# Start of a fused FFN, attention, FFN block: first block of tokens normalised alone, weight flag from raw bits, one branch instead of two

## The reference

```python
def _L0_ffn_ref(x, w1_w, w1_s, w2_w, w2_s, h1_w, h1_s, h2_w, h2_s, w3_w, w3_s):
    h = silu(_tlin(x, w1_w, w1_s)) * _tlin(x, w2_w, w2_s)      # 128 -> 512
    h = gelu(_tlin(h, h1_w, h1_s))                             # 512 -> 512
    h = gelu(_tlin(h, h2_w, h2_s))                             # 512 -> 512
    return _tlin(h, w3_w, w3_s)                                # 512 -> 128
x = x + 0.5 * ffn(layernorm(x))
x = x + attention(layernorm(x))        # 16 heads of 8, softmax over 256 keys
x = x + 0.5 * ffn(layernorm(x))
```

## Time and profile before

| What | us |
|---|---|
| three executions | 636.6, 638.17, 639.28 (median 638.17) |
| the profiled execution, its own time | 636.52 |
| its span | 634.7 |
| TensorE busy | 597.0 (94%) |
| ScalarE busy | 466.7 (74%) |
| VectorE busy | 436.8 (69%) |
| GpSimd busy | 94.7 (15%) |

### The profile page before, as it was taken

One profiled execution on the slowest core, in us unless ns is written; L12 is line 12 of the kernel. 1 busy time (PEld: TensorE's weight loads), 2 busy tenths in 40 slices (PEclk: granted clock), 3 DMA queues, 4 the chain that ended last, 5 costly groups with the idle time before them and its releaser, 6 DMA issues.

```text
span 634.7 us, 12980 instructions
## 1 busy us (share of the span) xinstructions
PE 597.0 (94%) x4452; PEld 437.7 (69%) x4452; DVE 436.8 (69%) x1034; ACT 466.7 (74%) x793; POOL 94.7 (15%) x258
## 2 busy tenths in 40 slices
PE   1959999999999999999999999999899999999996
PEld 0738878878776675656656565666578878788785
DVE  4845485667835687979889898896385666855742
ACT  2746796787875568787878878787587877977964
POOL 2702001021010311222222222012001020020000
PEclk9979999999999979999999999999899999999999
DMA  8200000000034073434437062400000001000011
GB/s 287 69 2 2 0 1 1 2 0 0 1 133 133 24 242 124 144 136 133 165 104 263 36 229 106 162 2 2 3 2 0 1 1 35 0 6 27 1 33 35
DMA packets 36674, 41.97 MB, mean 66 GB/s; under 512 B 2448, under 2 KB 27280, under 8 KB 36624
## 3 DMA queue, kind: packets, MB, share of 16 engines
q1 hardware_dynamic: 36624, 41.31, 19.3%
HBM read 22.42 MB, written 18.87 MB: 65 GB/s over the span
## 4 chain that ended last, share of the span: by engine, by line
PE 76%; DVE 8%; issue 7%; POOL 3%; ACT 3%; DMA 2%; POOLq 0%; SPq 0%; DVEq 0%; ACTq 0%
PE bank L1021 48%; PE bank L1129 7%; PE bank L1104 6%; PE bank L1116 3%; PE bank L1118 2%; DVE neg_max L832 2%; PE bank L1161 2%; PE bank L1086 1%; PE bank L1090 1%; DVE act_lo L782 1%; PE bank L1068 1%; PE bank L1147 1%; PE bank L1139 1%; DMA QK<-qk_scratch 1%; DVE silu L791 1%
## 5 line engine op out<-in xcount | busy, mean ns | idle before, releaser
L1021 PE MATMUL bank<-act_hi,WH 128*128 128x512 f32 x576 | 233.1, 405 | 6.6 <-issue 5.3
L1021 PE MATMUL bank<-act_lo,WH 128*128 128x512 f32 x576 | 228.3, 396 | 0.0
L832 DVE TENSOR_REDUCE neg_max<-bank 128x2 f32<-128x512 f32 x256 | 166.2, 680 | 31.8 <-PE bank L1104 30.2
L802 DVE TENSOR_TENSOR act_lo<-full,act_hi 128x512 fp32r<-128x512 f32 x128 | 87.8, 688 | 123.2 <-ACT act_hi L536 123.0
L647 ACT ACTIVATE probs<-bank 128x512 f32<-128x512 f32 x256 | 139.3, 597 | 34.1 <-PE bank L1118 32.3
L534 ACT ACTIVATE full<-bank,SG 128x512 f32<-128x512 f32 x128 | 88.1, 688 | 70.0 <-PE bank L1021 69.6
L1021 PEld LDWEIGHTS bank<-act_hi,WH 128*128 128x128 f32 x576 | 108.7, 189 | 36.8 <-issue 5.9
L1021 PEld LDWEIGHTS bank<-act_lo,WH 128*128 128x128 f32 x576 | 108.8, 189 | 25.1 <-issue 0.5
L1116 PE MATMUL bank<-QK 32*128 32x256 f32 x512 | 93.1, 331 | 0.9 <-DVE m_parts L838 0.5
L536 ACT ACTIVATE act_hi<-bank,SG 128x512 fp32r<-128x512 f32 x128 | 87.4, 683 | 0.0
L1118 PE MATMUL bank<-m_parts,SEL 32*128 32x256 f32 x512 | 79.3, 277 | 0.0
(11 more groups left out here) (91 smaller groups left out, 593.2 us busy)
## 6 DMA issues: line engine op xcount, KB each, us to landing
qk_scratch<-qk SPq DMA_DIRECT2D x64, 256.0 KB, 2.6
QK<-qk_scratch SPq DMA_DIRECT2D x16, 1024.0 KB, 7.1
X<-x SPq DMA_DIRECT2D x4, 512.0 KB, 7.2
raw_rest<-w_ffn SPq DMA_DIRECT2D x4, 512.0 KB, 6.0
out<-X SPq DMA_DIRECT2D x4, 512.0 KB, 3.2
raw<-w_ffn SPq DMA_DIRECT2D x3, 256.0 KB, 4.5
WA<-w_att SPq DMA_DIRECT2D x1, 256.0 KB, 5.4
xT<-sel SPq DMA_DIRECT2D x1, 256.0 KB, 5.4
```

The source lines that it names most:

```text
L802: D.tensor_tensor(act_lo[1 + layer][:, j, t, :], full[:, t, :], act_hi[1 + layer][:, j, t, :].bitcast(F32), op=ALU.subtract)\
L832: D.tensor_reduce(neg_max[:, bb, qt, n0:n0 + 2], bank[(banks or A_BANKS[bb])[u]][:, :].rearrange("p (h k) -> p h k", h=2), axis=AX.X, op=A ...
L1021: ins = MM(dst, a, b, start=k == 0, stop=k == len(todo) - 1)
```

## The change

1. **x in halves.** The first pair of x comes in two DMAs of 256 KB, `x_in` and `x_second_in`.
2. **Block 0 alone.** VectorE makes the statistics and the guess of block 0 (4 tiles of tokens), then runs its three Newton rounds itself (`first_newton`, 9 operations: the fused `scalar_tensor_tensor` does two of the four steps), with the statistics of block 1 written in between. GpSimd's Newton is for block 1 only. Block 1 is normalised after block 0's low part, and TensorE transposes it after the second tile of `layer1`.
3. **Flag from raw bits.** `low_bits(k)` takes the largest magnitude of the low 16 bits of each fp32 weight, read as int16 with a step of two, from the raw weights. It waits for the DMA of the group only. The matmul that sums it stands after tile 6 of `layer1`, ahead of tile 7.
4. **GpSimd's low parts later.** It starts them when 4 tiles of `act_lo` are made (`h_lo`), and ScalarE waits for them ahead of the second hidden layer. `raw_rest` moves to the place of that layer's output.
5. **ScalarE's order.** `weight_hi` of groups 2 and 3 comes ahead of block 0's `split_x`, groups 4 to 6 and block 1's `split_x` after it.
6. **One branch.** Both FFN phases and attention stand in one function, `all_layers`, written twice; the two-matmul form comes first, and the branch is not taken when the flag is 0.

```diff
-            load_x(0, x_in)
+            for j, arrived in ((0, x_in), (1, x_second_in)):
+                sp.dma_start(X[:, TT * j:TT * j + TT, :], x_t[:, TT * j:TT * j + TT, :]).then_inc(arrived, 16)
...
-            rsqrt_steps(0, 0)
+            rsqrt_steps(0, 0, TT, TT)
+            pool.wait_ge(h_lo, HT)
             for k in range(2, len(W_GROUPS)):
                 pool.wait_ge(w_hi, k + 1)
...
+                    if f == 0 and first:
+                        act.wait_ge(w_lo_rest, len(W_GROUPS) - 2)
                     hidden(g + 2 * HT, 1, 0)
...
                     weight_hi(0)
                     weight_hi(1)
+                    weight_hi(2)
+                    weight_hi(3)
                     split_x(nb, 0)
-                    weight_hi(2)
-                    split_x(nb + 1, 1)
-                    weight_hi(3)
+                    weight_hi(4)
                     act.wait_ge(consts_in, 16 * N_CONSTS)
-                    layer1(t1, {t: lambda k=t + 4: weight_hi(k) for t in range(3)})
+                    layer1(t1, {0: lambda: weight_hi(5), 1: lambda: split_x(nb + 1, 1), 2: lambda: weight_hi(6)})
...
-            def weight_lo_max(k):
-                if k < 2:
-                    dve.wait_ge(w_lo, k + 1)
-                else:
-                    dve.wait_ge(w_lo_rest, k - 1)
-                D.tensor_reduce(lo_max[:, k:k + 1], part_of(WL, k).bitcast(F32), axis=AX.XY, op=ALU.max,
-                                apply_absolute_value=True).then_inc(lo_reduced, 1)
+            def low_bits(k):
+                dve.wait_ge(w_in[k], 16)
+                halves = raw_of(k).bitcast(I16).rearrange("p k (c t) -> p k c t", t=2)
+                D.tensor_reduce(low_max[:, k:k + 1], halves[:, :, :, 0], axis=AX.XY, op=ALU.max,
+                                apply_absolute_value=True).then_inc(bits_reduced, 1)
...
+            def first_newton(it, step):
+                v, y, a = var_m[:, 0:TT], rstd[:, 0:TT], newton[:, 0:TT]
+                if it == 0 and step == 0:
+                    dve.wait_ge(first_guess, 1)
+                else:
+                    dve.wait_ge(first_step, 3 * it + step)
+                if step == 0:
+                    ins = D.tensor_tensor(a, y, y, op=ALU.mult)
+                elif step == 1:
+                    ins = D.tensor_tensor(a, a, v, op=ALU.mult)
+                else:
+                    ins = D.scalar_tensor_tensor(out=y, in0=a, scalar=1.5, in1=y, op0=ALU.add, op1=ALU.mult)
+                ins.then_inc(first_rstd if (it, step) == (NEWTON - 1, 2) else first_step, 1)
...
-                    side = {t: lambda k=t + 2: weight_lo_max(k) for t in range(5)}
-                    layer1(t1, side | {5: all_lo_max, 6: take_flag})
+                    layer1(t1, {0: lambda: low_bits(3), 1: lambda: low_x(nb + 1, 1), 2: lambda: low_bits(4),
+                                3: lambda: low_bits(5), 4: lambda: low_bits(6), 5: all_low_bits, 6: take_flag})
...
+            def all_layers(general):
+                pe.wait_ge(w_hi, len(W_GROUPS))
+                if general:
+                    pe.wait_ge(w_lo_rest, len(W_GROUPS) - 2)
+                ffn_bodies(0, general)
...
+                ffn_bodies(1, general)
...
+            transpose_x(0, 0)
+            pe.wait_ge(w_lo, 2)
+            layer1(0, 0, True, {1: lambda: transpose_x(1, 1), 6: sum_low_bits})
+            pe.wait_ge(flag_set, 1)
+            pe.reg_load(low_weights, flag[0:1, 0:1].bitcast(I32))
+            with pe.If_eq(low_weights, 0):
+                all_layers(False)
+            with pe.Else():
+                all_layers(True)
```

More of the change, by code:

```diff
@@ L24 @@
 F32R = mybir.dt.float32r
+I16 = mybir.dt.int16
 I32 = mybir.dt.int32
@@ L156, in macaron_kernel @@
         x_in = sem("x_in")
+        x_second_in = sem("x_second_in")
         x_rest_in = sem("x_rest_in")
@@ L730, in take_flag, with norm_steps @@
                 D.tensor_copy(flag[:, :], bank[6][0:1, 0:1]).then_inc(flag_set, 1)
-            def norm_steps(n, tile0, width=8, biased=0):
+            def norm_steps(n, tile0, width=8, biased=0, at=0, sems=None):
+                done = sems or (stats_done, moments_done, var_done, half_done, guess_done)
+                cols = slice(at, at + width)
                 def s_stats():
@@ L755, in s_half @@
+                    D.tensor_scalar(var_m[:, cols], moments[:, cols, 1], EPS, -0.5, ALU.add, ALU.mult)
+                    D.tensor_scalar(var[:, cols], moments[:, cols, 1], EPS, None, ALU.add).then_inc(done[2], 1)
                 def s_half():
-                    dve.wait_ge(var_done, n + 1)
-                    D.tensor_scalar(half[:, 0:width], var[:, 0:width].bitcast(I32), 1, None,
-                                    ALU.arith_shift_right).then_inc(half_done, 1)
+                    dve.wait_ge(done[2], n + 1)
@@ L760, in s_guess @@
+                    D.tensor_scalar(half[:, cols], var[:, cols].bitcast(I32), 1, None,
+                                    ALU.arith_shift_right).then_inc(done[3], 1)
                 def s_guess():
-                    dve.wait_ge(half_done, n + 1)
-                    D.tensor_scalar(rstd[:, 0:width].bitcast(I32), half[:, 0:width], -1.0,
-                                    float(RSQRT_MAGIC), ALU.mult, ALU.add).then_inc(guess_done, 1)
+                    dve.wait_ge(done[3], n + 1)
+                    D.tensor_scalar(rstd[:, cols].bitcast(I32), half[:, cols], -1.0,
+                                    float(RSQRT_MAGIC), ALU.mult, ALU.add).then_inc(done[4], 1)
@@ L769, in normalise @@
+            def normalise(n, tile0, t0, width=4, ready=None):
+                dve.wait_ge(ready or rstd_done, n + 1)
                 for t in range(t0, t0 + width):
@@ L1244, in ffn_bodies, with sum_low_bits @@
                 body(NP - 1, more=False)
[L1246 to L1270 removed]
+            def sum_low_bits():
+                pe.wait_ge(ones_set, 1)
+                pe.wait_ge(bits_reduced, len(W_GROUPS) + 1)
+                MM(bank[6][0:1, 0:1], ONES[:, 0:1], low_max[:, len(W_GROUPS):len(W_GROUPS) + 1],
+                   start=True, stop=True).then_inc(flag_sum, 1)
             def attend(b, pair, par, bb, prev=True, prev2=True, own=True, more=True, steps=UNITS,
@@ L1351, in att_body @@
                 attend(2 * i + 1, i, par, 1, prev2=not first, more=more, ahead=i + 2 if ahead else None)
-            att_body(0, 0, first=True)
-            att_body(1, 1)
-            with pe.Fori(1, NPAIR // 2 - 1) as n:
-                att_body(2 * n, 0)
-                att_body(2 * n + 1, 1)
-            att_body(NPAIR - 2, 0, ahead=False)
-            att_body(NPAIR - 1, 1, ahead=False, more=False)
-            attend(NBATCH, NPAIR, 0, 0, own=False, more=False, steps=SKEW + 4)
-            ffn_phase(1, low_weights)
+            def all_layers(general):
[3 more added lines that the diff above has]
+                ffn_bodies(0, general)
+                att_body(0, 0, first=True)
+                att_body(1, 1)
+                with pe.Fori(1, NPAIR // 2 - 1) as n:
+                    att_body(2 * n, 0)
+                    att_body(2 * n + 1, 1)
+                att_body(NPAIR - 2, 0, ahead=False)
+                att_body(NPAIR - 1, 1, ahead=False, more=False)
+                attend(NBATCH, NPAIR, 0, 0, own=False, more=False, steps=SKEW + 4)
+                ffn_bodies(1, general)
+            low_weights = T.alloc_register("low_weights")
+            pe.wait_ge(eye_in, 16)
+            transpose_x(0, 0)
[7 more added lines that the diff above has]
+                all_layers(True)
 def kernel(**inputs):
```

104 lines of the change are left out of this document (54 added, 50 removed).

## The result

| | before | after |
|---|---|---|
| median of 19 executions each, us | 637.89 | 639.46 |
| lowest and highest | 635.2, 639.28 | 637.63, 643.23 |
| span of the profiled execution | 634.7 | 637.2 |
| TensorE busy | 597.0 | 600.6 |
| VectorE, ScalarE, GpSimd busy | 436.8, 466.7, 94.7 | 440.7, 467.5, 95.5 |

The changed kernel takes 1.0036 of the time of the one before, 95% interval 1.0020 to 1.0052: 0.4% slower, which is less than the 0.5% that counts as a difference here. 627.0 was forecast, in a range of 623.8 to 632.0. So some 12 us are missing.

The account below looks back on a forecast made before the run. TensorE, busy for 94% of the span, was taken as the bound, so only its stops and half clock could give time: 2.7 + 4.5 + 1.9 + 1.55 = 10.65 us off 636.52 gives 625.9, placed against the mean as 627.0; range 623.8 to 632.0.

Parts of the forecast that it names:

- Branch not taken: TensorE's flag branches: falling through to the next instruction avoids far jumps, at the loops' price of 0.08 to 0.24 us.
- costs at nothing: GpSimd's later low parts, block 1's scaling and the general code's jump at TensorE's end were all counted as hidden.
- a nonzero flag: Rival: a nonzero low half read sends TensorE through the general code, 321 us more, about 948 us; chance 0.02.
- start, S: First weight matmul on TensorE: 2.7 us earlier, near 13.3 in place of 15.98; bounds 2.3 to 2.8.
- flag, H - S: First weight matmul to first matmul behind the branch: 19.7 us in place of 24.27, gain 4.5; bounds 3.3 to 5.7.
- clock in the first hidden tile: TensorE behind the first branch: full clock stays, eight matmuls take 1.86 us in place of 3.77; gain 1.9, bounds 0 to 1.9.
- second branch: Ahead of the second FFN on TensorE: the branch goes, and its 1.56 us stop with it; gain 1.55, bounds 1.3 to 2.4.
- the rival of the slow reduce: VectorE's int16 reduce at double price delays the flag some 5 us and the clock falls: 634 us; chance 0.08.
- The jump at the end: Behind TensorE's last transposes: a far jump of up to 3.6 us over the general code, hidden with 0.9 us of cover.
- The stall is not from the jump: Rival: a branch on a freshly loaded register costs 3.5 us whichever way it goes; about 631 us; chance 0.08.
- The start gives little: Rival: half of x lands no sooner, weight copies delay the high part; start 1.2 us earlier, 628.5 us; chance 0.12.

Follow-up runs that it names:

- e1: The changed kernel with 32 increments of an unused semaphore on TensorE ahead of its first transposes: 629.12 us, 0.9869 of before.
- e8: The e1 kernel with GpSimd's low parts begun when tile 7 of the hidden layer is written rather than tile 4: 625.33 us, 0.9816 of before.
- e5: The kernel before with only TensorE's one branch over the whole program in place of one per layer: 630.49 us, 0.9879 of before.
- e9: The e1 kernel without the wait that holds back GpSimd's low parts, so that they run early: 633.58 us, 0.9947 of before.
- e10: The e5 kernel with a single semaphore increment ahead of TensorE's first transposes: 640.77 us, 1.0065 of before.
- e7: The changed kernel with each layer's feed-forward again behind its own branch, the rest of the change kept: 637.20 us, 0.9989 of before.

## Why the prediction was wrong

**The step that failed** is the one called "Branch not taken", with the one on costs at nothing. It took the move of the general code to be free but for the far jump at the end, and let the rest of the program run as before. The rows had the warning in them: the earlier trace rows shows that a jump back costs 76 to 243 ns and a far jump 3.4 us, which reads as a cheap jump to code that is there and one of 3 to 4 us to code that isn't. I used that for the two branches, and did not ask of the attention loop, 57 us long, on which side of this it stands and by what margin. It stood at the margin. Cost: 9.8 us on the profiled execution, 10.3 between e1 and after. No rival had it. The one that ended slower was a nonzero flag, which did not occur: both profiles have 4452 matmuls.

The rest of the sum can be read off e1, the change with its loop kept whole: 629.12 us, inside the range, against 627.0. Its profiled span is 7.8 us shorter than before's, where 10.65 was the sum:

| Term | forecast | e1 | e8 |
|---|---|---|---|
| start, S | 2.7 | 3.3 | 3.5 |
| flag, H - S | 4.5 | 1.2 | 4.3 |
| clock in the first hidden tile | 1.9 | 1.7 | 1.7 |
| from there to the attention loop | 0 | -0.8 | -0.8 |
| second branch | 1.55 | 2.6 | 2.7 |
| sum, with roundings | 10.65 | 7.8 | 11.3 |

Each is the difference of the same starts as in the table of the result. e5 has the branch alone and a span 6.0 us shorter than before's (628.7). So the start and the flag's earlier time add 1.8 us in e1 and 5.3 in e8, though S alone is 3.3 earlier.

- **Start: right, a little short.** Statistics of block 0 began at 3.79, not at 4.65: half of x came sooner than I put it, and below the range for it. The last Newton operation started at 8.3 and the scaling ended at 9.58. From there S took 2.96 us in place of 2.72, and the slack of 1 us that I gave ScalarE wasn't there: the chain goes through a weight copy at 10.13 that waited for its DMA.
- **Flag: the reduce was right, the low parts were not.** 1024 int16 halves take 1.21 us, as the fp32 numbers did, so the rival of the slow reduce falls. The row I took for a low part beside GpSimd had 1.12 us; it measured 2.52 and 2.12. The wait ahead of tile 7 was 1.8 us longer for it (3.2 against e8's 1.37), and around this wait the clock fell to half (0.83 at 30 to 33 us, 0.60 at 33 to 36; e8 has 1.00), so that tile 7 took 3.5 us in e1 (32.29 to 35.78) and 2.0 in e8 (30.43 to 32.46). Together 3.3 us, the whole difference between e1's H and e8's. I had priced the collision by one row in which the two engines met only in part. In e8 H - S is 20.0, where 19.7 was forecast; its whole gain over e1 is 3.8 us by the medians and 3.5 by the spans.
- **What the Trainium skill says of this.** The Trainium skill ("SBUF — State Buffer", Who interferes with whom) says that VectorE and GpSimd share a pair of ports as an exclusive lock, so that a VectorE operation with two SBUF inputs waits out a GpSimd one. For act_lo with its two inputs the rows agree: 2.5 us, the length of one GpSimd subtraction (10.73 / 4 = 2.7). The scaling of block 1 in e9 has one tile as input and two columns of scalars, and waited as well; the same section counts tensor_scalar among the operations that can take the shared pair. On the reduce, the Trainium skill ("VectorE: DVE Perf Modes", The perf-mode tier table) has only the plain rate for tensor_reduce, and 1.21 us for either type agrees.
- **Clock: the size was right in e1 and e8, the reason was not.** The prediction took from the earlier trace rows that a stop of 1.56 us leaves the clock whole. That row begins at 454. Ahead of the stop the clock was already at half, and it rose during the stop:

```profile
451.00:452.00 1.00, 1.00 (x10) 0.45 (x13) 0.42 (x1) 0.38 (x1) 0.00 (x0) 0.50 0.00 0
```

  In the changed kernel itself the clock was at half from about 31 us to 37, and the first hidden tile and its wait took 5.7 us (H to the second tile), against 6.4 before and 4.8 in e1.
- **From there to the attention loop: 0.8 us that no step had.** In the changed kernel the clock is at half from 218.2 to 228.5 us, 10.2 us long, before it was from 224.9 to 231.7, 6.8 long. It isn't the start's doing: e5, with the branch alone, has the 10.2 us too and loses 0.7, and e10, one increment further, has 6.8 and loses 0.1. Why the stretch is longer in some is open.
- **Second branch: right, short by 1.** The idle row of 1.56 us was not all that the branch cost, since the 16 matmuls queued ahead of it ran at half clock: 1.94 us, where e1 has 1.07. In e7, which has the branch and full clock at that place, they take 1.07 and the stop is 2.60 us; from the first of them to the first matmul of the layer it is 3.67 us there and 3.49 before, against 1.00 in e1. So a jump hidden in part behind slow matmuls was priced by its idle row:

```profile
453.16 0.47 PE L1073 MATMUL bank<-x_hi,WH 128*128 128x512 f32 x1 [2.60 <-issue]
```

- **The jump at the end: right.** 3.71 us from 632.0 in the changed kernel, and the span ends with the last store; it costs nothing that shows.
- **Rivals.** "The stall is not from the jump" falls by 93 ns in place of 3579. The Trainium skill's 108 ns ("Advanced Engine Details and Errata", Control Flow Timing), cited in the prediction, is near that branch, which isn't taken, and far from the jumps of 3.3 to 3.75 us. "The start gives little" falls by S.
- **Range and chances.** The range spanned the terms of the sum. 0.93 for faster was given on traces that show only what the change touches, and left nothing for code that it moves.

## What to carry to other kernels

An edit that adds, removes or moves instructions moves all the code behind it, and a long loop may stop being kept whole: look at the duration of its branch and at the instruction fetches of its second pass, before and after, before you read anything else from a comparison of two kernels. Here one instruction was worth 10.3 us, more than any part of the change; a version that looks bad can be a good one in a bad place, and a few idle instructions in a place where the engine waits anyway tell which. When GpSimd works, price the VectorE operations of the two kinds seen here to wait, a subtraction of two SBUF tiles and a scaling, at the length of GpSimd's (the SiLU product, with one operand in PSUM, kept its 0.73 us), and put GpSimd's work where nothing on VectorE is waited for.

## What the runs showed of the hardware

- The jump back of the attention loop takes 0.2 us where its second pass fetches no code or one block, and 4.6 to 5.1 us where it fetches nine. In the changed kernel another stop of 2.18 us and half clock (0.50 at 337 to 343 us) follow. The second pass is 9.8 to 11.7 us longer in the four kernels that stall.
- A loop that fetches its code six times in its first pass (0.10 MB) ran its second without a fetch in before and e5. The Trainium skill ("Advanced Engine Details and Errata", ISA Cache) gives TensorE 128 KB and 16 KB lines and then says "Only 2 cache lines!". By two lines no such loop could be kept; the runs speak against it, and are at ease with the 128 KB, eight lines by the figures of that section (an estimate).
- The Trainium skill ("Runtime: NRT & Kernel Launch", Instruction fetch mechanics) says that a taken jump outside of a window of two pages forces a fetch before execution goes on. The far jumps agree, with 3.3 to 3.75 us against 0.09 for the one that isn't taken. The window of two doesn't: the loop's jump back over six fetches of code took 0.2 us.
- Increments of a semaphore by TensorE follow each other at 0.15 us: 32 of them last until 5.7 us, 192 until 30.2.
- Beside GpSimd's subtractions a VectorE subtraction of two SBUF tiles took 2.1 to 2.5 us in place of 0.68, and four scalings 8.13 in place of 1.1; the SiLU product, with one operand in PSUM, kept 0.73.
